# Four block-diagonal score products issued as 32-row tiles side by side, in the landmark phase of a hybrid ConvLSTM and attention layer

## What is computed

```python
x = x + conv_lstm_2d(group_norm(x))               # 16 x 64 x 64 x 128
t = tokens(x)                                     # 16 x 4096 x 128
xn = layer_norm(layer_norm(t)) * gamma + beta
q, k, v = split(xn @ w_qkv)                       # 8 heads of 16
q_l, k_l = means of q, k over 64 tokens           # 64 landmarks
attn1 = softmax(q @ k_l.T); attn2 = softmax(q_l @ k_l.T)
attn3 = softmax(q_l @ k.T)                        # 64 landmarks x 4096 tokens, a head
out = attn1 @ pinv(attn2) @ (attn3 @ v) + depthwise_conv(v)
t = layer_norm(t) + out @ w_out + b_out           # then a recurrent layer over the tokens
```

## Time and profile before

| | us |
|---|---|
| median of 3 runs | 6150.85 (6145.19 to 6154.91) |
| the profiled execution, its time | 6144.53 |
| its span, first to last instruction | 6142.9 |
| landmark phase, from the trace, about | 1521 to 2473 |
| mean granted TensorE clock | 0.974 of full speed |

### The profile page before, as it was taken

One profiled execution on the slowest core, in us unless ns is written; L12 is line 12 of the kernel. 1 busy time (PEld: TensorE's weight loads), 2 busy tenths in 40 slices (PEclk: granted clock), 3 DMA queues, 4 the chain that ended last, 5 costly groups with the idle time before them and its releaser, 6 DMA issues. The chain is left out here.

```text
span 6142.9 us, 243622 instructions
## 1 busy us (share of the span) xinstructions
PE 5658.1 (92%) x102096; PEld 3377.5 (55%) x102096; DVE 2953.6 (48%) x7658; ACT 3195.0 (52%) x9222; POOL 1816.5 (30%) x2146
## 2 busy tenths in 40 slices
PE   5599999997899998789999997999999999999999
PEld 4499888996666665654455444333333333333333
DVE  8577666774777775558888886000000000000000
ACT  5455555564666665358888885333333333333333
POOL 2000000002877774248888886000000000000000
PEclk7799999998999999999999998999999999999999
DMA  8721111225777773347777775011111211111111
GB/s 350 284 106 62 56 56 63 76 84 182 236 232 229 218 229 103 94 131 219 219 220 221 217 221 148 26 45 47 45 47 46 60 45 47 45 47 45 47 47 44
DMA packets 857511, 758.02 MB, mean 123 GB/s; under 512 B 71024, under 2 KB 732528, under 8 KB 853360
## 3 DMA queue, kind: packets, MB, share of 16 engines
q1 hardware_dynamic: 840784, 640.78, 35.0%
q0 software_dynamic: 14208, 101.45, 4.1%
q10 hardware_dynamic: 1440, 0.33, 0.0%
HBM read 425.72 MB, written 308.45 MB: 120 GB/s over the span
## 5 line engine op out<-in xcount | busy, mean ns | idle before, releaser
L2512 PE MATMUL f_junk<-f_idle 128*32 128x384 bf16 x24736 | 1566.5, 323 | 2.1 <-issue 2.0
L2555 ACT ACTIVATE f_y<-f_acc 128x16 f32<-128x16 f32 x4096 | 753.7, 184 | 1551.8 <-PE f_acc L2523 1551.8
L2523 PEld LDWEIGHTS f_acc<-f_y,f_vT 128*32 128x32 f32 x32768 | 649.0, 108 | 1411.8 <-ACT f_y L2555 1400.4
L2523 PE MATMUL f_acc<-f_y,f_vT 128*32 128x16 f32 x32768 | 1049.5, 193 | 57.7 <-issue 8.9
L2470 DVE TENSOR_TENSOR f_sum<-f_turned,f_t 128x512 f32<-128x512 f32 x128 | 88.5, 691 | 1765.4 <-PE f_turned L2505 1765.3
L2512 PEld LDWEIGHTS f_junk<-f_idle 128*32 128x32 bf16 x24736 | 447.2, 96 | 4.3 <-issue 4.2
L2230 DVE TENSOR_REDUCE o_m<-o_bank_l 128x8 f32<-128x512 f32 x512 | 329.1, 684 | 185.7 <-PE o_bank_l L2008 184.3
L533 POOL DMA_DIRECT2D hidden<-l_h x48 | 36.1, 754 | 1199.1 <-DVE l_hsum L733 972.7
L1170 ACT ACTIVATE a_p<-a_s 128x512 f32<-128x512 f32 x512 | 264.2, 603 | 149.5 <-PE a_s L1055 149.5
L656 ACT ACTIVATE l_gate<-l_pf,l_bf 128x256 f32<-128x256 f32 (+7 forms) x512 | 202.2, 446 | 239.6 <-PE l_pf L583 215.1
L2188 ACT ACTIVATE o_p<-o_bank_s 128x512 f32<-128x512 f32 x512 | 264.3, 602 | 84.8 <-PE o_bank_s L2029 84.8
(11 more groups left out here) (280 smaller groups left out, 11911.4 us busy)
## 6 DMA issues: line engine op xcount, KB each, us to landing
o_v<-vals SPq DMA_DIRECT2D x256, 272.0 KB, 3.4
a_hid<-hidden SPq DMA_DIRECT2D x112, 520.0 KB, 4.7
hidden<-l_h POOLq DMA_DIRECT2D x48, 1040.0 KB, 6.4
skew<-gn_skew POOLq DMA_DIRECT2D x8, 6144.0 KB, 23.5
l_x<-skew SPq DMA_DIRECT2D x46, 1024.0 KB, 5.2
vals<-a_v SPq DMA_DIRECT2D x128, 272.0 KB, 3.4
gn_x<-in_x SPq DMA_DIRECT2D x16, 2048.0 KB, 16.9
a_xin<-in_x SPq DMA_DIRECT2D x128, 256.0 KB, 4.6
```

Of the source, the lines that this page charges most:

```text
L2512: nc.tensor.matmul(junk[rows, :], idle[:, 0:QUAD], idle[:, :], start=True, stop=True)
L2523: mm = nc.tensor.matmul(acc[k % 2][rows, t, :], vT[:, rows], before, start=False, stop=True, skip_group_check=True)
L2555: nc.scalar.activation(y[q][:, u, :], acc[u // RC % 2][:, u % RC, :], ACT.Sigmoid).then_inc(s_y, 1)
```

## The change

A new function takes the place of the loop over four calls of `rounded_scores` in PE's slot. It waits once, ahead of all four: for the rounded key chunk that the last of the four needs, and for the count of `mx` that each of the four waited for before. Each product then reads only the 32 rows of its head pair in both operands, so that four products with four different row groups follow each other, each into its own bank. Only the last adds to `lp`, by 4. Products into `L` still go through `rounded_scores`, over 128 rows. DVE, ACT, POOL and SP are as before; DVE's first maximum of the four waits for `lp` as before, which now reaches its count with the last product.

```diff
+            def four_rounded_scores(i, first, free):
+
+                wait(pe, "rk", NG * i + (first + PAIRS_H - 1) // PAIRS_H + 1)
+                if first == 0:
+                    wait(pe, "set", SET * i + 7)
+                wait(pe, "mx", free)
+                for k in range(PAIRS_H):
+                    j = first + k
+                    g = j % PAIRS_H
+                    rows = slice(QUAD * g, QUAD * g + QUAD)
+                    mr = nc.tensor.matmul(S[k][:, :], qbd_lp[rows, P * g:P * g + P], k_lp[j // PAIRS_H % 3][rows, :],
+                                          start=True, stop=True)
+                mr.then_inc(s["lp"], PAIRS_H)
...
                 if maxima:
                     if valid(p - 2):
                         wait(pe, "exp", PAIRS_H * nth(p - 2, c))
-                    for g in range(PAIRS_H):
-                        rounded_scores(p - 1, four - PAIRS_H + g, S[g], NL * (p - 1) + (spread(c - 1)[1] if c - 1 in SLOTS else 0))
+                    four_rounded_scores(p - 1, four - PAIRS_H, NL * (p - 1) + (spread(c - 1)[1] if c - 1 in SLOTS else 0))
```

## The result

The changed kernel takes 6166.55 us (median of 13 runs, 6159.15 to 6177.31) against 6146.23 (13 runs, 6137.38 to 6154.91): slower by 20 us, ratio 1.0037 with a 95% interval of 1.003 to 1.0044. The forecast was 8.7 us faster, the range 6133 to 6156. It was wrong in sign and in range.

The account below looks back on a forecast made before the run. PE, DVE and ACT handing each other every slot's work was taken as the bound. Steady periods 6.7 us plus period 16 2.0 us made 8.7 us off the median: 6142.2 us, range 6133 to 6156.

Parts of the forecast that it names:

- The chains: Two loops setting slot time: PE with ACT 6.75 us; DVE 7.04 in slots 2 to 4, 6.57 in 5 and 6.
- the pack: Four 32-row products on PE take 0.22 us, or 0.32 with the following change of shape, instead of 0.97.
- the margins: Spare time before DVE's maxima wait for the last product: slot 2 0.11 us, slots 3-4 0.53, slots 5-7 0.06.
- the slots that could gain: Slot 2 gains 0.12 us, slots 5 and 6 0.18 each: 0.48 a steady period, 6.7 us over 14.
- The waits ahead: PE needs the key chunk earlier: costs nothing; in period 1 bounded at 0 to 0.8 us once, taken as 0.
- The change of shape: On PE, transposes over 128 rows before products over 32 cost 0.10 us, paid in slot 2.
- PE's waits for maxima ahead of the scores: Sign to look for on PE: these waits rise from two a period to five, 0.4 to 0.6 us each.
- the row: Profile row of the scores' first products, same shape and banks: 0.22 us to the next group; taken over the skill's 3.07 times.
- Period 16: Last period, without new tokens: gain of 2.0 us, between -1 and 2.6.
- part 2: DVE in slots 2 to 7: its work is unchanged, so only 0.48 us a steady period is gained, 6.7 in all.
- Slot 7: nothing: Slot 7 gains 0 us, since its end is DVE's maxima, softmax and merge without a gap.
- Part 7: Last period: more PE idle time may keep the clock at 1.2 of 2.4 GHz one more slot, some 0.6 us.

Follow-up runs that it names:

- six products in the wait: Kernel before with six unread bf16 products added into bank L in slot 0, ahead of the transpose of the maxima: ratio 1.0.
- the late count: Changed kernel with the four products over all 128 rows again, keeping the waits ahead and the one add to lp at the end: ratio 1.006.
- both moved: Changed kernel and kernel before, each with slot 0's weighted sums and values put ahead of the transpose of the maxima: ratios 0.9991 and 0.998.
- three kernels of four: Slot 0 work put ahead of the transpose: before, sums and values 0.998; changed, sums 0.9981; before, sums 0.9979. Fourth: changed, sums and values 0.9991.
- before again: Kernel before, unedited, profiled a second time: ratio 1.0001.
- changed again: Changed kernel, unedited, profiled a second time: ratio 1.0043 to the kernel before.

## Why the prediction was wrong

The chains, the pack and the margins held. PE's saving is 0.64 a slot (0.65 to 0.75 forecast), the slots that could gain gained 0.39 to 0.43 a period (0.48 forecast), and DVE's start didn't move. The waits ahead cost nothing in the steady periods; in period 1, PE waited 0.65 us for the rounded keys ahead of one pack, inside the bound of 0.8. The change of shape ahead of the pack costs its 0.10 in slot 2: from the four transposes at 1888.69 to the pack at 1889.28 it is 0.59, before 0.49. PE's waits for maxima ahead of the scores, in the stretch from 1640 to 2380 us, went up as forecast; before, then after:

```profile
PE a_s L1049 <- DVE a_m3p L1230: 5.9, 26, 0.2
```
```profile
PE a_s L1063 <- DVE a_m3p L1243: 37.9, 63, 1.0
```

The pack's 0.33 is the row's value with the change of shape behind it, 0.32. The factor of 3.07 that the Trainium skill gives ("TensorE: Matmul & The Clock Gate", Measured speedup vs the span model) makes 0.32 without that change. With it, by estimate, the time to the next group would be about 0.42, and DVE's starts in slots 5 to 7 don't show the 0.04 that it would have cost. Here the row was right.

One term of the sum was too large, which alone wouldn't have changed the sign. Period 16 was to give 2.0 us. The last interval between transposes went from 55.92 and 55.51 (the two traces of the kernel before) to 55.32 and 55.30, so it gave 0.2 to 0.6. With the clock up in its slot 0, the kernel before needed only 52.72 there (six products in the wait).

The step that failed is in part 2: "Slot 7: nothing", and "PE's other 0.5 us a slot turns into idle time before the scores, for DVE". Idle time was costed at zero wherever another engine ended the wait. In slot 7 the pack lengthened PE's idle stretch ahead of the maxima from 1.85 to 2.17 in the median, and what followed it, 2.2 us of PE work that stands on the way in slot 0, then ran near half clock: +1.54. With the 0.4 that the slots gave, a period went from 56.9 to 58.0. Part 7 named just this mechanism, but only for period 16, and priced it at 0.6. Even without falls the gain would have been some 6 us, too small for the times here to show.

The trace had the warning. In the earlier trace rows the transposes of line L1036 have a longest of 474 ns beside a median of 328. The transpose of period 16, which ends the steady periods, had 2.28 us of idle time ahead, and behind it the values took 1.92:

```profile
2384.77 0.47 PE L1036 MATMUL a_l<-r_ident,a_m 128*128 128x128 f32 x1 [2.28 <-DVE a_m L1266]
2385.04 1.92 PE L1005 MATMUL a_proj<-a_w,a_xnT 128*128 128x128 f32 x8
```

One interval was 58.15, with the clock low in slot 0. I had read both as odd ones out. A stretch of 1.84 us that was mostly fine and one of 2.28 that was not should have made a rival: "the clock falls in slot 0", with a price of 14 times 1.55 less 6.7, some +15 us.

What stays open: 20 us were measured, and the traces show 4 to 11 us more from first to last transpose, plus 2 to the end of the phase. The rest can lie in how many slots fell in the profiled executions (the kernel before had 2 falls in one and 6 in the other) and in the later stages, where the first pair of traces has 20 us more and the second none. The kernel with the late count, slower by 14 to 18 us more than its transposes show and without a fall, and the pair with both moved point to a part outside slot 0 that no run here explains.

## What to carry over

Before taking work off PE, look at its longest idle stretch and at what stands behind it: time won ahead of a wait is not merely worthless, it can cost the clock of the work after the wait. Compare such stretches within one trace, those followed by a full clock and those that were not; if some were not, the fall is a rival with a price. If PE has to wait there anyway, real work moved into the wait can be worth more than the change itself: here 11 to 12 us in three kernels of four. And compare a version without falls with another one without falls.

## What the runs showed beyond that

The length of the idle stretch shifts how often the clock falls, over a few tenths of a microsecond. In four traces whose stretch ahead of the transpose has a median of 1.85 or 1.86 us it fell 2, 6, 1 and 0 times of 14 (before, before again, tiles in slots 2 to 6, late count). In three traces with medians of 2.17 to 2.45 (changed, changed again, slot 7 alone) it fell 13, 11 and 10 times. Three products, 0.65 us, ahead of what was left of the stretch were enough for none in 14. But the length doesn't decide the single case: with tiles in slot 7 alone the clock stayed up behind stretches of 2.40 and twice 2.49 us, and before again it fell behind 1.84.

DVE's product for attn2 took 1.15 us in both kernels (median) and 0.54 in the one with the late count, where it ran at another time against POOL: before, in the period of the earlier trace rows, it started 0.18 us after a step of POOL of 1.04 us (L943), there 0.79 us after it. That only suggests that the two engines got in each other's way; it wasn't tried.
